# A routed expert loop that takes four lanes through each stage instead of two

## The chip, the cores and the metric

The kernel runs on one core of a Trainium2 chip. The metric is the time of one execution on the device in microseconds; the compared value is the median of several runs.

## The reference

One transformer layer on x of [2, 1024, 512]: attention with 32 query heads and 8 key heads, then a mixture of 64 routed experts with four chosen per token, and two shared experts. The feed-forward part is

```python
logits = flat @ router_w                                  # 2048 tokens, 64 experts
_, topk_idx = jax.lax.top_k(logits + router_bias, 4)
comb = ...                                                # renormalised softmax scores of the four
g = jax.nn.silu(jnp.einsum('nd,edf->nef', flat, wg))      # d = 512, f = 128
u = jnp.einsum('nd,edf->nef', flat, wu)
routed = jnp.einsum('ne,nef,efd->nd', comb, g * u, wd)
sg = jax.nn.silu(jnp.einsum('nd,sdh->nsh', flat, swg))    # two shared experts, h = 512 each
su = jnp.einsum('nd,sdh->nsh', flat, swu)
shared = jnp.einsum('nsh,shd->nd', sg * su, swd)
return routed + shared
```

## The kernel before

Each engine has its own program, written out by hand, and they meet in semaphores. Up to about 640 us the kernel does attention, the router and the shared experts for the first half of the tokens (`shared_ups`, `shared_down` for g = 0, 1). Then comes the routed loop, then the shared experts for the second half (g = 2, 3), while the routed results are fetched and mixed in.

**The lanes.** The choices (token, expert) are sorted by expert into tiles of 64 slots. There are 8 lanes of 24 tiles; a lane walks through its tiles and keeps its expert's weights while the expert stays the same. Two lanes form a pair (j = 0 to 3), side by side in the 128 partitions: each lane's weights are loaded as 64 columns of TensorE's array. Pair number n = 4 i + j runs from 0 to 95.

**The stages of pair n**, with the lines of the kernel before:
- GpSimd gathers its tokens (L919, `gather_tokens`, one indirect DMA), with slot numbers that ScalarE copied (L1097, `next_tokens`).
- TensorE turns them (`turn_slots`, L1443 and L1444, eight matmuls with full 128x128 weights); ScalarE copies the result (L1084, `turned_tokens`).
- TensorE multiplies by gate and up weights (`expert_up`, L1483, fp32, eight calls that are recorded as sixteen matmuls, with 64-column weights); ScalarE applies silu (L1089), VectorE the product (L1863, `expert_hidden`); ScalarE and VectorE split it into two fp16 parts (L1094 `e_high`, L1867 `e_low`).
- TensorE turns both parts (`turn_hidden`, L1492 and L1493, two matmuls with 128x128 weights); ScalarE copies (L1103, `hidden_turned`).
- The down weights are scaled and split: high part on ScalarE (L1109, `down_high`), low part on VectorE (L1873, `down_low`), in two buffers, `[:, j % 2]`. TensorE multiplies (`expert_down`, L1502, six matmuls with 64-column weights).
- VectorE takes the result out (L1880, L1882, `expert_y`) and GpSimd scatters it (L928, `scatter_y`, one indirect DMA, eight pairs behind the gather it follows).
- SyncE loads the weights of pair n + 4 into a buffer when up(n) and down_low(n) have read it (L645, L653).

**The order on the engines** is that of `expert_pairs` in each program. Before, a turning is one pair. TensorE: slots(n+1), hidden(n-2), up(n), down(n-2). ScalarE: turned(n+1), hidden_turned(n-2), next_tokens, down_high(n-1), silu(n), e_high(n). VectorE: expert_hidden(n), down_low(n-1), e_low(n), expert_y(n-2).

**Behind the loop** TensorE does `shared_up(g, hc)`, number k = 8 g + hc, 24 matmuls of 512 columns (L1360); from k = 17 on each waits for the hidden product k - 2 of VectorE (L1808). VectorE's order there is hidden(k), hidden_low(k-1), `mix(k - 16)` (L1911), where mix(t) waits for the routed results of token tile t, which SyncE fetches when all scatters have landed (L677).

## Time and profile before

| | us |
|---|---|
| Median of 3 runs | 1092.0 |
| Lowest, highest run | 1090.39, 1092.01 |
| The profiled execution's own time | 1091.62 |
| Its span, first to last instruction | 1089.8 |
| TensorE busy in the span | 1041.6 |
| VectorE, ScalarE, GpSimd busy | 848.8, 660.8, 532.5 |

The profile holds one execution. Times in it count from the span's start. A matmul's recorded length is that of its way through the array, so matmuls overlap in the records, and an engine that streams them looks busy throughout; starts, or the pieces of the chain, tell how fast the stream runs.

### The profile page before, as it was taken

Reading aid. Unit: us, or ns where it says so; the run is one execution under the profiler, and the core shown is the slowest. Engines: PE = TensorE matmul, PEld = TensorE weight load, DVE = VectorE, ACT = ScalarE, POOL = GpSimd, SP = SyncE. Lnnn points to the kernel's source line nnn. Section 1 sums busy time; section 2 is a strip of 40 time slices with the busy share of each in tenths; the row PEclk is TensorE's granted clock in tenths of the full one; section 3 lists DMA queues with packets and bytes.
Section 4 is the critical chain, followed back from the end, with each engine's and each line's share of the span. In section 5 each row is a group of like instructions: output and inputs, shape, how many; then the busy total and the mean of one; then the engine's idle time right before and its main releaser. Section 6 shows DMA issues by size and latency. Waiting matters only on the chain.

```text
span 1089.8 us, 29733 instructions
## 1 busy us (share of the span) xinstructions
PE 1041.6 (96%) x9832; PEld 504.8 (46%) x9833; DVE 848.8 (78%) x1331; ACT 660.8 (61%) x1334; POOL 532.5 (49%) x540
## 2 busy tenths in 40 slices
PE   5998899999999999899999999999999999989998
PEld 3534333333333333345544456666666666634443
DVE  6976999999999997398878927676777777768283
ACT  3323788888888889735620317777777777722020
POOL 6631143334333433435881946777777888610000
PEclk9998999999999999999999999999999999999999
DMA  9164111121112110044200077888887798558261
GB/s 260 26 170 107 43 49 46 46 73 58 44 45 73 58 44 25 6 150 155 78 1 1 2 270 247 270 265 280 304 288 238 231 317 293 177 194 268 67 226 39
DMA packets 72409, 150.66 MB, mean 138 GB/s; under 512 B 19460, under 2 KB 20868, under 8 KB 72356
## 3 DMA queue, kind: packets, MB, share of 16 engines
q1 hardware_dynamic: 52404, 109.51, 31.7%
q0 software_dynamic: 18304, 38.86, 10.9%
q10 hardware_dynamic: 1648, 1.58, 0.4%
q8 instruction: 35, 0.57, 0.2%
q14 instruction: 18, 0.15, 0.0%
HBM read 223.90 MB, written 38.80 MB: 241 GB/s over the span
## 4 chain that ended last, share of the span: by engine, by line
PE 71%; DVE 17%; issue 7%; ACT 3%; DMA 1%; POOL 1%; DVEq 0%; SPq 0%; ACTq 0%; POOLq 0%
PE PS L1483 17%; PE PS L1360 13%; PE PS L1465 8%; DVE maxes L1558 7%; PE PS L1502 6%; PE PS L1274 5%; PE PS L1223 4%; DVE max_low L1558 4%; PE PS L1155 4%; PE PS L1443 3%; PE PS L1252 3%; ACT att L1004 2%; PE PS L1327 2%; PE PS L1444 2%; DVE XT L1737 1%
## 5 line engine op out<-in xcount | busy, mean ns | idle before, releaser
L1004 ACT ACTIVATE att<-PS 128x512 f32<-128x512 f32 x576 | 312.6, 594 | 51.2 <-PE PS L1252 44.3
L1274 PE MATMUL PS<-att,v_head 128*32 128x256 f32 (+1 forms) x2560 | 178.2, 369 | 0.9 <-POOL att L793 0.9
L1558 DVE TENSOR_REDUCE maxes<-PS 128x2 f32<-128x1024 f32 (+2 forms) x192 | 172.6, 939 | 1.2 <-PE PS L1160 1.1
L1360 PE MATMUL PS<-XN,att 128*128 128x512 f16 x768 | 167.8, 380 | 0.3 <-ACT w_att L1066 0.3
L1558 DVE TENSOR_REDUCE max_low<-PS 128x2 f32<-128x1024 f32 x128 | 153.1, 1208 | 5.2 <-PE PS L1155 3.1
L919 POOL DMA_INDIRECT w_att<-xn_rows,idx x96 | 117.9, 1229 | 46.9 <-DVE w_att L1882 12.4
L793 POOL TENSOR_SCALAR_AFFINE_SELECT att<-att 128x512 f32<-128x512 f32 (+1 forms) x96 | 75.1, 790 | 127.8 <-ACT att L1004 127.0
L1252 PE MATMUL PS<-att 50*128 50x512 f16 (+1 forms) x640 | 111.7, 362 | 14.2 <-ACT att L1004 11.8
L1155 PE MATMUL PS<-att 48*128 48x512 f16 (+7 forms) x768 | 115.8, 325 | 9.0 <-DVE max_low L1558 3.9
L1360 PEld LDWEIGHTS PS<-XN,att 128*128 128x128 f16 x768 | 74.9, 98 | 91.2 <-issue 2.1
L1062 ACT ACTIVATE w_att<-PS 128x512 f32<-128x512 f32 x32 | 19.1, 598 | 158.3 <-PE PS L1360 158.3
L1863 DVE TENSOR_TENSOR w_att<-w_att,PS 128x128 f32<-128x128 f32 x96 | 27.6, 288 | 89.9 <-ACT w_att L1089 88.0
L1483 PE MATMUL PS<-XT,w_att 128*64 128x256 f32 x768 | 93.5, 385 | 0.2 <-issue 0.2
L1483 PE MATMUL PS<-ring,w_att 128*64 128x256 f32 x768 | 93.5, 385 | 0.1
L1155 PEld LDWEIGHTS PS<-att 48*128 48x128 f16 x768 | 35.7, 93 | 117.3 <-DVE maxes L1558 53.9
L1274 PEld LDWEIGHTS PS<-att,v_head 128*32 128x32 f32 x2560 | 55.9, 108 | 72.9 <-issue 48.4
L1465 PE MATMUL PS<-att,XT 128*128 128x512 f16 x384 | 83.7, 379 | 0.0
L1502 PE MATMUL PS<-XT,w_att 128*64 128x512 f16 x576 | 79.2, 382 | 1.9 <-DVE XT L1873 1.9
L1084 ACT ACTIVATE w_att<-PS 128x512 f32<-128x512 f32 x96 | 57.4, 597 | 39.0 <-PE PS L1444 33.7
L928 POOL DMA_INDIRECT choice_y<-w_att,idx_y x48 | 63.2, 1318 | 19.7 <-issue 8.3
L928 POOL DMA_INDIRECT choice_y<-att,idx_y x48 | 60.0, 1250 | 20.5 <-issue 8.6
L759 POOL TENSOR_TENSOR small<-small,recip 128x256 f32<-128x256 f32 x32 | 19.9, 621 | 93.5 <-DVE recip L1631 93.5
(205 smaller groups left out, 1827.5 us busy)
## 6 DMA issues: line engine op xcount, KB each, us to landing
ring<-in_L_ffn_wg_dram SPq DMA_DIRECT2D x96, 512.0 KB
XT<-in_L_ffn_wg_dram SPq DMA_DIRECT2D x96, 512.0 KB
ring<-in_L_ffn_wd_dram SPq DMA_DIRECT2D x96, 256.0 KB
XT<-in_L_ffn_wd_dram SPq DMA_DIRECT2D x96, 256.0 KB
ring<-choice_y SPq DMA_DIRECT2D x16, 1024.0 KB, 6.2
att<-q_stacks SPq DMA_DIRECT2D x60, 128.0 KB, 2.5
xn_rows<-ring SPq DMA_DIRECT2D x16, 256.0 KB, 3.1
out_dram<-X SPq DMA_DIRECT2D x16, 256.0 KB, 6.1
```

The costliest lines, as they stand in the source:

```text
L793: pool.affine_select(out=d, in_=d, compare_op=ALU.is_ge, fill=0.0, base=0, pattern=[[0, n], [1, P]], channel_multiplier=-1).then_inc(maske ...
L919: pool.indirect_dma_start(out=xg[:, j, :], out_offset=None, in_=xn2_rows[:, :], in_offset=bass.IndirectOffsetOnAxis(ap=idx[:, j:j + 1], ax ...
L928: pool.indirect_dma_start(out=choice_y[:, :], out_offset=bass.IndirectOffsetOnAxis(ap=idx_y[:, j:j + 1], axis=0), in_=result[j], in_offset ...
L1004: act.activation(probs[:, n0 % RING, u * BANK:(u + 1) * BANK], bank((2 * n0 + u) % EXP_BANKS), ACT.Exp, scale=HD ** -0.5 / QK_SCALE ** 2). ...
L1155: mm = pe.matmul(PS[:, to:to + n], q_max[b][rows, t * P:(t + 1) * P], k_max[b][rows, first:first + n], start=True, stop=lo is not None)
L1252: mm = pe.matmul(PS[:, at:at + 2 * qn], k_exp[b][rows, kt * P:(kt + 1) * P], q_exp[b][rows, 2 * q0:2 * (q0 + qn)] .rearrange("p (t h q) -> ...
L1274: mm = pe.matmul(PS[32 * r:32 * r + 32, at:at + qn], v_head[b][:, kt, :], probs[:, (NS * b + s) % RING, a:a + qn], start=s in (0, NS0), st ...
L1360: mm = pe.matmul(bank(2 * (n % 2) + k), shared_w[:, 2 * k + w, C * s + c, at:at + P], v[:, c, tokens], start=(c == 0 and w == 0 and v is x ...
L1465: mm = pe.matmul(bank(4 + t % 2), v[:, hc, (t % 4) * P:(t % 4 + 1) * P], swd_w[:, w, hc, :], start=(hc == 0 and w == 0 and v is hidden_hi) ...
L1483: mm = pe.matmul(PS[l * SUB:(l + 1) * SUB, at:at + 2 * F], xgt[:, j % 2, c * P + l * SUB:c * P + (l + 1) * SUB], lane_up[2 * j + l][:, :, ...
L1502: mm = pe.matmul(PS[l * SUB:(l + 1) * SUB, (4 + j % 2) * BANK:(5 + j % 2) * BANK], hg[:, j % 2, v * P + l * SUB:v * P + (l + 1) * SUB], w[ ...
L1558: last = dve.reduce_max(out, src, AXX)
```

## The change

The unit of `expert_pairs` becomes two pairs, a and a + 1, on TensorE, ScalarE and VectorE. TensorE turns the slots of a + 2 and a + 3, then both hidden parts of a - 2 and a - 1, then does both ups of a and a + 1 and both downs of a - 2 and a - 1. Slots 0 and 1 are turned ahead of the loop. The split down weights have four buffers, `[:, j]`, which lie in the first half of x_hi and x_lo (tile XN), whose tokens the shared experts have used by then; the waits for a free buffer go from e_down n - 1 to n - 3. `next_tokens` asks for pair n + 6, not n + 5. On ScalarE, down_high(a) ends a turning and down_high(a - 1) stands behind the two hidden_turned at its start. On VectorE both down_low of the turning before come first. After the last up and down of the loop, TensorE does the first shared block, `shared_up(EARLY, 0)`, ahead of the last turn_hidden of 94 and 95; `shared_ups` for g = 2 then begins with its second block. The programs of GpSimd and SyncE are untouched.

The diff, cut to its core:

```diff
...
         pair_down = [carve(arena, at, [P, 2, D])[0]
 -        down_hi, down_lo = carve_all(flat_xt, 2 * W, *[([P, 2, 2 * D], F16)] * 2)
+        down_hi, down_lo = x_hi[:, :, 0:2 * D], x_lo[:, :, 0:2 * D]
         xg, xgt, yb, sg, ht, hg = carve_all(w_att, 0, ([P, 4, 2 * D], F16), ([P, 2, D], FP32), ([P, 2, D], FP32),
                                             ([P, 2, P], FP32), ([P, 2, P], FP32), ([P, 2, 2 * P], F16))
         ht_hi, ht_lo = carve_all(w_att, 4 * D + 2 * D + 2 * D + 6 * P, ([P, 2, P], F16), ([P, 2, P], F16))
...
             def down_high(n, j, i):
                 act.wait_ge(pair_down_in[j], 32 * (i + 1))
 
-                wait(act, e_down, n - 1)
-                act.activation(down_hi[:, j % 2, :], pair_down[j][:, :, :].rearrange("p l d -> p (l d)"), ACT.Copy,
+                wait(act, e_down, n - 3)
+                act.activation(down_hi[:, j, :], pair_down[j][:, :, :].rearrange("p l d -> p (l d)"), ACT.Copy,
                                scale=W_SCALE).then_inc(down_hi_done, 1)
 
-            def expert_pairs(i, first, last):
-                for j in range(JP):
-                    n = JP * i + j
-                    if not (last and j == JP - 1):
-                        turned_tokens(n + 1, j + 1)
-                    if not (first and j < 2):
-                        hidden_turned(n - 2, (j - 2) % JP)
-                    if not last:
-                        next_tokens(i + 1 + (j + 1) // JP, (j + 1) % JP)
-                    if not (first and j < 1):
-                        down_high(n - 1, (j - 1) % JP, i if j else i - 1)
-                    silu(n, j)
-                    e_high(n, j)
+            def expert_pairs(i, first, turns, gathers):
+                for a in range(0, JP, 2):
+                    both = (a, a + 1)
+                    if not (first and a == 0):
+                        for j in both:
+                            hidden_turned(JP * i + j - 2, (j - 2) % JP)
+                        down_high(JP * i + a - 1, (a - 1) % JP, i if a else i - 1)
+                    for j in both:
+                        n = JP * i + j
+                        silu(n, j)
+                        if a < turns:
+                            turned_tokens(n + 2, j + 2)
+                        if a < gathers:
+                            next_tokens(i + 1 + (j + 2) // JP, (j + 2) % JP)
+                        e_high(n, j)
+                    down_high(JP * i + a, a, i)
 
             act.wait_ge(table_ready, 1)
             for j in range(JP):
                 next_tokens(0, j)
-            turned_tokens(0, 0)
-            next_tokens(1, 0)
-            expert_pairs(0, True, False)
-            with act.Fori(1, LANE_TILES - 1) as i:
-                expert_pairs(i, False, False)
-            expert_pairs(LANE_TILES - 1, False, True)
-            hidden_turned(PAIRS - 2, JP - 2)
-            hidden_turned(PAIRS - 1, JP - 1)
+            for j in range(2):
+                turned_tokens(j, j)
+                next_tokens(1, j)
+            expert_pairs(0, True, JP, JP)
+            expert_pairs(1, False, JP, JP)
+            with act.Fori(2, LANE_TILES - 2) as i:
+                expert_pairs(i, False, JP, JP)
+            expert_pairs(LANE_TILES - 2, False, JP, JP - 2)
+            expert_pairs(LANE_TILES - 1, False, JP - 2, 0)
+            for j in (JP - 2, JP - 1):
+                hidden_turned(PAIRS - JP + j, j)
             down_high(PAIRS - 1, JP - 1, LANE_TILES - 1)
 
             act.wait_ge(e_down, PAIRS)
...
                     if t == 4 * EARLY - 1:
                         pe.wait_ge(table_ready, 1)
                         pe.wait_ge(ident_h_set, 1)
-                        turn_slots(0, 0, 0)
+                        for n in range(2):
+                            turn_slots(n, n, 0)
                     if t == 4 * EARLY:
                         pe.wait_ge(yb_ready, PAIRS)
                     if t >= 2:
...
                     for l in range(2):
                         mm = pe.matmul(PS[l * SUB:(l + 1) * SUB, (4 + j % 2) * BANK:(5 + j % 2) * BANK],
                                        hg[:, j % 2, v * P + l * SUB:v * P + (l + 1) * SUB],
-                                       w[:, j % 2, l * D:(l + 1) * D], start=(v == 0 and w is down_hi), stop=v == 1)
+                                       w[:, j, l * D:(l + 1) * D], start=(v == 0 and w is down_hi), stop=v == 1)
                 mm.then_inc(e_down, 1)
 
             def expert_pairs(i, first, last):
-                for j in range(JP):
-                    n = JP * i + j
-                    if not (last and j == JP - 1):
-                        turn_slots(n + 1, j + 1, i)
-                    if not (first and j < 2):
-                        turn_hidden(n - 2, (j - 2) % JP)
-                    expert_up(n, j, i)
-                    if not (first and j < 2):
-                        expert_down(n - 2, (j - 2) % JP)
+                for a in range(0, JP, 2):
+                    both = (a, a + 1)
+                    if not (last and a == JP - 2):
+                        for j in both:
+                            turn_slots(JP * i + j + 2, j + 2, i)
+                    if not (first and a == 0):
+                        for j in both:
+                            turn_hidden(JP * i + j - 2, (j - 2) % JP)
+                    for j in both:
+                        expert_up(JP * i + j, j, i)
+                    if not (first and a == 0):
+                        for j in both:
+                            expert_down(JP * i + j - 2, (j - 2) % JP)
 
 
             expert_pairs(0, True, False)
             with pe.Fori(1, LANE_TILES - 1) as i:
                 expert_pairs(i, False, False)
             expert_pairs(LANE_TILES - 1, False, True)
-            turn_hidden(PAIRS - 2, JP - 2)
-            turn_hidden(PAIRS - 1, JP - 1)
-            expert_down(PAIRS - 2, JP - 2)
-            expert_down(PAIRS - 1, JP - 1)
+            pe.wait_ge(xgt_ready, PAIRS)
+            pe.wait_ge(x_lo_ready, 4 * (EARLY + 1))
+            shared_up(EARLY, 0)
+            for j in (JP - 2, JP - 1):
+                turn_hidden(PAIRS - JP + j, j)
+            for j in (JP - 2, JP - 1):
+                expert_down(PAIRS - JP + j, j)
 
             for g in range(EARLY, 4):
-                shared_ups(g, g % EARLY)
+                shared_ups(g, 1)
                 shared_down(g)
 
         @block.vector
...
 
             def down_low(n, j):
                 dve.wait_ge(down_hi_done, n + 1)
-                wait(dve, e_down, n - 1)
-                dve.scalar_tensor_tensor(out=down_lo[:, j % 2, :], in0=pair_down[j][:, :, :].rearrange("p l d -> p (l d)"),
-                                         scalar=W_SCALE, in1=down_hi[:, j % 2, :], op0=ALU.mult, op1=ALU.subtract)\
+                wait(dve, e_down, n - 3)
+                dve.scalar_tensor_tensor(out=down_lo[:, j, :], in0=pair_down[j][:, :, :].rearrange("p l d -> p (l d)"),
+                                         scalar=W_SCALE, in1=down_hi[:, j, :], op0=ALU.mult, op1=ALU.subtract)\
                    .then_inc(down_lo_done, 1)
 
             def expert_y(n, j, i):
...
                 dve.wait_ge(e_down, n + 1)
                 dve.tensor_scalar(result[j], bank(4 + j % 2), 1 / (H_SCALE * W_SCALE), None, ALU.mult).then_inc(yb_ready, 1)
 
-            def expert_pairs(i, first, last):
-                for j in range(JP):
-                    n = JP * i + j
-                    expert_hidden(n, j)
-                    if not (first and j < 1):
-                        down_low(n - 1, (j - 1) % JP)
-                    e_low(n, j)
-                    if not (first and j < 2):
-                        expert_y(n - 2, (j - 2) % JP, i if j >= 2 else i - 1)
-
-            expert_pairs(0, True, False)
-            expert_pairs(1, False, False)
-            with dve.Fori(2, LANE_TILES - 1) as i:
-                expert_pairs(i, False, False)
-            expert_pairs(LANE_TILES - 1, False, True)
-            down_low(PAIRS - 1, JP - 1)
-            expert_y(PAIRS - 2, JP - 2, LANE_TILES - 1)
-            expert_y(PAIRS - 1, JP - 1, LANE_TILES - 1)
+            def expert_pairs(i, first):
+                for a in range(0, JP, 2):
+                    later = not (first and a == 0)
+                    n, before = JP * i + a, i if a else i - 1
+                    if later:
+                        down_low(n - 2, (a - 2) % JP)
+                        down_low(n - 1, (a - 1) % JP)
+                    expert_hidden(n, a)
+                    e_low(n, a)
+                    expert_hidden(n + 1, a + 1)
+                    if later:
+                        expert_y(n - 2, (a - 2) % JP, before)
+                    e_low(n + 1, a + 1)
+                    if later:
+                        expert_y(n - 1, (a - 1) % JP, before)
+
+            expert_pairs(0, True)
+            expert_pairs(1, False)
+            with dve.Fori(2, LANE_TILES) as i:
+                expert_pairs(i, False)
+            for j in (JP - 2, JP - 1):
+                down_low(PAIRS - JP + j, j)
+            for j in (JP - 2, JP - 1):
+                expert_y(PAIRS - JP + j, j, LANE_TILES - 1)
 
             def mix(t):
```

TensorE in the steady loop, before: behind the last matmul of turn_slots (L1443, L1444) come turn_hidden (L1492, L1493), up (L1483), down (L1502), and the next slots.

```order
L1444 MATMUL PS<-ident_h,w_att 128x128
L1492 MATMUL PS<-ident_h,w_att 128x128
L1493 MATMUL PS<-ident_h,w_att 128x128
L1478 REGISTER_ALU
L1483 MATMUL PS<-XT,w_att 64x256 x8
L1502 MATMUL PS<-XT,w_att 64x512 x6
L1438 ISA
L1443 MATMUL PS<-ident_h,w_att 128x128
```

The same place after, where turn_slots is L1449 and L1450, turn_hidden L1499 and L1500, up L1490, down L1509:

```order
L1450 MATMUL PS<-ident_h,w_att 128x128
L1499 MATMUL PS<-ident_h,w_att 128x128
L1500 MATMUL PS<-ident_h,w_att 128x128
L1499 MATMUL PS<-ident_h,w_att 128x128
L1500 MATMUL PS<-ident_h,w_att 128x128
L1490 MATMUL PS<-XT,w_att 64x256 x16
L1509 MATMUL PS<-XN,w_att 64x512 x12
L1531 REGISTER_ALU
L1531 COMPARE_AND_BRANCH
L1449 MATMUL PS<-ident_h,w_att 128x128
```

Two ups stand in a row, and two downs; between one change of the weights' width and the next there is twice the work.

ScalarE in the steady loop, before: turned_tokens (L1084), hidden_turned (L1103), next_tokens (L1097), down_high (L1109), silu (L1089), e_high (L1094), one pair.

```order
L1084 ACTIVATE w_att<-PS 128x512
L1103 ACTIVATE w_att<-PS 128x256
L1097 ISA
L1097 ACTIVATE idx<-small 128x1
L1109 ACTIVATE XT<-XT 128x1024
L1089 ACTIVATE w_att<-PS 128x128
L1094 ACTIVATE w_att<-w_att 128x128
```

The same lines after, one turning of two pairs:

```order
L1103 ACTIVATE w_att<-PS 128x256 x2
L1109 ACTIVATE XN<-ring 128x1024
L1089 ACTIVATE w_att<-PS 128x128
L1081 REGISTER_ALU
L1084 ACTIVATE w_att<-PS 128x512
L1097 ISA
L1097 ACTIVATE idx<-small 128x1
L1094 ACTIVATE w_att<-w_att 128x128
L1089 ACTIVATE w_att<-PS 128x128
```

Turned_tokens has moved behind silu and ahead of e_high, and both hidden_turned and one down_high stand at the start of the turning.

TensorE at the loop's end, before: the last up (L1483), the downs, both turn_hidden, and then the shared blocks (L1360).

```order
L1483 MATMUL PS<-XT,w_att 64x256 x8
L1502 MATMUL PS<-XT,w_att 64x512 x6
L1492 MATMUL PS<-ident_h,w_att 128x128
L1493 MATMUL PS<-ident_h,w_att 128x128
L1492 MATMUL PS<-ident_h,w_att 128x128
L1493 MATMUL PS<-ident_h,w_att 128x128
L1502 MATMUL PS<-XT,w_att 64x512 x12
L1360 MATMUL PS<-XN,att 128x512 x216
```

The same place after, where the shared blocks are L1366:

```order
L1490 MATMUL PS<-XT,w_att 64x256 x16
L1509 MATMUL PS<-XN,w_att 64x512 x12
L1366 MATMUL PS<-XN,att 128x512 x24
L1499 MATMUL PS<-ident_h,w_att 128x128
L1500 MATMUL PS<-ident_h,w_att 128x128
L1499 MATMUL PS<-ident_h,w_att 128x128
L1500 MATMUL PS<-ident_h,w_att 128x128
L1509 MATMUL PS<-XN,w_att 64x512 x12
L1366 MATMUL PS<-XN,att 128x512 x192
```

One shared block of 24 matmuls now stands between the last downs and the last turn_hidden.

## Rows read from the trace of the kernel before

**Rows 1.** The page, busy us of an engine, share of the span, instructions.
```profile
PE 1041.6 (96%) x9832; PEld 504.8 (46%) x9833; DVE 848.8 (78%) x1331; ACT 660.8 (61%) x1334; POOL 532.5 (49%) x540
```

**Rows 2.** Table by stretch, the routed loop: length, busy (x instructions), clock, DMA.
```profile
core 0: us, PE busy (x) PEld busy (x) DVE busy (x) ACT busy (x) POOL busy (x), PEclk, DMA share, GB/s
655.00:950.00 295.00, 294.69 (x2943) 183.13 (x2940) 209.88 (x459) 229.53 (x551) 228.04 (x181) 1.00 0.79 267
```

**Rows 3.** Chain of work that ended last, in the loop: start, us, what.
```profile
943.17 0.18 PE PS L1443
943.35 0.06 PE PS L1444
...
943.86 1.88 PE PS L1483 x16
945.73 0.65 PE PS L1502 x6
...
947.06 1.88 PE PS L1483 x16
...
947.86 1.08 PE PS L1483 x10
```

**Rows 4.** Timeline of ScalarE, in the loop and at its end: start, us, line.
```profile
759.35 0.28 ACT L1089 ACTIVATE w_att<-PS 128x128 f32<-128x128 f32 x1
759.98 0.31 ACT L1094 ACTIVATE w_att<-w_att 128x128 f16<-128x128 f32 x1 [0.35 <-DVE w_att L1863]
760.55 0.60 ACT L1084 ACTIVATE w_att<-PS 128x512 f32<-128x512 f32 x1 [0.27 <-PE PS L1444]
761.05 0.38 ACT L1103 ACTIVATE w_att<-PS 128x256 f16<-128x256 f32 x1
761.41 1.06 ACT L1109 ACTIVATE XT<-XT 128x1024 f16<-128x1024 f32 x1
...
954.93 0.28 ACT L1089 ACTIVATE w_att<-PS 128x128 f32<-128x128 f32 x1 [0.56 <-PE PS L1483]
```

**Rows 5.** Timeline of VectorE, in the loop.
```profile
758.06 0.68 DVE L1882 TENSOR_SCALAR att<-PS 128x512 f32<-128x512 f32 x1
759.66 0.29 DVE L1863 TENSOR_TENSOR w_att<-w_att,PS 128x128 f32<-128x128 f32 x1 [0.92 <-ACT w_att L1089]
759.86 1.22 DVE L1873 SCALAR_TENSOR_TENSOR XT<-ring,XT 128x1024 f16<-128x1024 f32 x1
761.00 0.28 DVE L1867 SCALAR_TENSOR_TENSOR w_att<-w_att 128x128 f16<-128x128 f32 x1
...
761.26 0.68 DVE L1882 TENSOR_SCALAR w_att<-PS 128x512 f32<-128x512 f32 x1
```

**Rows 6.** Timeline of GpSimd, in the loop.
```profile
757.73 1.04 POOL L928 DMA_INDIRECT choice_y<-att,idx_y  x1 [0.31 <-issue]
759.16 1.03 POOL L919 DMA_INDIRECT w_att<-xn_rows,idx  x1 [0.39 <-DVE att L1882]
760.49 1.48 POOL L928 DMA_INDIRECT choice_y<-att,idx_y  x1 [0.31 <-issue]
```

**Rows 7.** Waits by engine, 670 to 940 us: total, times, longest.
```profile
ACT XT L1109 <- DMA ring<-in_L_ffn_wd_dram: 0.2, 1, 0.2
```

**Rows 8.** Timeline of TensorE at the loop's end.
```profile
954.72 0.82 PE L1502 MATMUL PS<-XT,w_att 128*64 128x512 f16 x6
...
956.92 0.23 PE L1492 MATMUL PS<-ident_h,w_att 128*128 128x128 f16 x1 [1.17 <-DVE w_att L1867]
...
959.89 1.49 PE L1502 MATMUL PS<-XT,w_att 128*64 128x512 f16 x6 [1.91 <-DVE XT L1873]
961.31 14.01 PE L1360 MATMUL PS<-XN,att 128*128 128x512 f16 x61
```

**Rows 9.** Timeline of VectorE behind the loop.
```profile
961.42 0.69 DVE L1882 TENSOR_SCALAR att<-PS 128x512 f32<-128x512 f32 x1 [0.87 <-PE PS L1502]
...
970.54 3.12 DVE L1911 SCALAR_TENSOR_TENSOR X<-ring,small,X 128x512 f32<-128x512 f32 x4 [1.66 <-DMA ring<-choice_y]
973.58 0.68 DVE L1808 SCALAR_TENSOR_TENSOR w_att<-PS,w_att 128x512 f32<-128x512 f32 x1
```

1 line of the change is left out of this document (removed).

## The prediction

> **What bounds the kernel now.** I read the page first: TensorE is busy for 1041.6 us of the 1089.8 us span [rows 1]. A share over the whole span says little of one stage, so the second view is the table by stretch. In the routed loop, 655 to 950 us, TensorE shows 294.7 us busy of 295 at a granted clock of 1.00, while VectorE has 210, ScalarE 230 and GpSimd 228 [rows 2]. The third view is the chain of work that ended last. There the loop is nothing but TensorE, pair after pair, 3.20 us apart (943.86 to 947.06) [rows 3].
>
> "Busy" is not "working", and the chain shows how much is not. In the chain a piece ends where the matmul ends, so a piece of one matmul is its share of the stream. Ten up matmuls in mid-stream take 1.08 us, thus 0.216 us for two (the two lanes run side by side). Sixteen should take 1.73 us, but where they follow the square 128x128 matmuls of turn_slots and turn_hidden they take 1.88: 0.15 us extra. The six of expert_down, which follow up with three waits of their own, take 0.65 = 3 x 0.216: nothing extra. The first square matmul after them takes 0.18 us where the nine others take 0.06: 0.12 us extra [rows 3]. So each pair pays 0.27 us for two changes: square to half-width (64-column) weights, and back. It does not pay for waits: turn_hidden has two waits of its own and goes on at 0.06. The loop's minimum is 3.21 - 0.27 = 2.94 us a pair.
>
> **What the change does to TensorE in the loop.** It removes no matmul. Two pairs share one turning: slots, slots, hidden, hidden, up, up, down, down. Each turning has one change to half width and one back, so 48 turnings have 48 double changes where 96 pairs had 96. That takes away 48 x 0.27 = 13.0 us, if TensorE never waits; the turning is then 2 x 3.207 - 0.27 = 6.14 us.
>
> **Does it wait?** I lay the other engines against a turning, with t = 0 at the start of up(a). TensorE: up(a) to 1.78, up(a+1) to 3.50, both downs to 4.80, both slots from 4.90 to 5.82, turn_hidden(a) at 5.82, turn_hidden(a+1) at 5.93, next turning at 6.14. Durations are those of [rows 4, 5]; ScalarE and VectorE start an instruction some 0.1 us before the recorded end of the one before; a releaser costs 0.03 (silu ends at 759.63, expert_hidden starts at 759.66); and silu starts 0.2 us after the matmul that follows its up (954.72 on TensorE in rows 8, 954.93 on ScalarE).
> - The chain that now matters: silu(a+1) at 3.70, turned_tokens(a+3) 3.89, the index copy 4.40, e_high(a+1) 4.51 to 4.82, e_low(a+1) 4.94 to 5.22. TensorE wants it at 5.93. It has 0.7 us of room. expert_y(a-2) stands ahead of e_low(a+1), but waits only for the first down (ends 4.15) and starts at 4.35.
> - ScalarE behind it: down_high(a) 4.73 to 5.79, two hidden_turned from 6.13 to 6.79, down_high(a+1) to 7.76; silu(a+2) is released at 8.11. Room 0.35 us.
> - VectorE: down_low(a+1) is released at 7.79 and runs to 9.01, so expert_hidden(a+2), queued behind it, starts 0.5 us late (8.92 instead of 8.42). e_high(a+2) follows at 9.24, and ScalarE would have waited until 9.83 for silu(a+3) anyway: nothing is passed on. down_low(a+1) itself is wanted at 10.28.
> - Slots(a+5) wait for turned_tokens(a+3), ready at 4.49, wanted at 5.37.
>
> So all waits keep some room and the stage stays TensorE's. The wait for down's buffers is gone with four of them, but it was not what bound anything: no row shows it.
>
> **GpSimd and the transfers.** GpSimd is the engine I trust least. A gather or scatter takes 1.03 to 1.04 us and 0.31 between two; a scatter over whose end expert_y runs takes 1.48 [rows 6]. It ends when expert_y ends: 761.97 against 761.94 (rows 5 and 6). Yet the scatter at 757.73 holds an expert_y wholly inside (758.06 to 758.74) and takes 1.04. So expert_y holds up only an end. Per turning: 4 x 1.34 = 5.36 us, plus at most two ends held, 0.45 each as in the row, 6.26. The two expert_y now end within 0.85 us of each other (5.03 and 5.87), so two ends, which are 1.34 apart, can hardly both be held: 5.8 us of 6.14. Next_tokens now asks for n+6 instead of n+5, so a gather late by 1 us still lands before it is turned. I take nothing for it.
>
> Weights: down_low(a) frees its buffer some 3.5 us later than now, so down weights have less lead. The one wait for them in the loop is 0.2 us [rows 7]. I take 0, and up to +3 us as the upper bound (the two busiest bursts losing 1.5 us each).
>
> **The start.** One more pair of slots stands ahead of up(0), which only moves work. But the first turning has no downs to cover the chain of ScalarE: slots(5) must wait for turned_tokens(3), which by the same calendar is ready 0.2 + 0.19 + 0.60 us after up(1), with 0.1 + 0.47 of slots(4) ahead of it: 0.5 us. The next up waits 0.2 us for turn_hidden(1). +0.7.
>
> **The end.** Before: TensorE waits 1.2 us for e_low(95) (recorded idle 1.17) and 1.9 us for down_low(95) (1.91) [rows 8]. After these the granted clock falls to half: the last six downs take 1.49 us where those at 954.72 take 0.82, +0.67, and the first 61 shared matmuls 14.01 where 61 x 0.216 + 0.16 = 13.3, +0.7. Together 4.5 us. After: shared_up(16), 24 matmuls of 0.216 = 5.2 us, fills the first wait. But ScalarE's down_high(95) stands behind both hidden_turned, and these now come after the shared block. From the last turn_hidden to the last expert_down it was 2.97 us (956.92 to 959.89); with one hidden_turned more it is 3.2, of which TensorE works 1.0. So 2.3 us of waiting are still there, 0.4 ahead of down(94) and 1.9 ahead of down(95), and with 0.3 for the shorter last turning it is 2.6.
>
> Then a new wait. Shared_up(19) needs hidden(17), which VectorE computes after mix(0), and mix(0) needs the last scatter. From the last expert_y's start (961.42) it is 9.1 us to mix(0) (970.54) and 12.2 to hidden(17) (973.58, ends 974.26) [rows 9]. After the change, with D the start of down(95), expert_y(95) starts at D + 0.84, and hidden(17) ends at D + 13.7 to 14.1 (0.4 if the scatter of 94 is in the way). TensorE meanwhile is one block further than before: it stands before shared_up(19) at D + 0.75 + 2 x 5.18 = 11.1. It waits 3.0 us there. VectorE catches up later: about 4.5 us of work per block against 5.2. Last, some 3 us of idle time halved the clock before at a cost of 1.4 us; I take that once more: +1.4.
>
> **Sum**, against the profiled execution's 1091.6 us (span 1089.8 and 1.8 around it): -13.0 in the loop, +0.7 at its start, -4.5 + 2.6 at its end, +3.0 at shared_up(19), +1.4 for the clock: -9.8, thus 1081.8 us. The runs' median, 1092.0, lies 0.4 above the profiled one.
>
> **Rivals.**
> 1. **The 0.27 belongs to the stages, not to the changes.** If each first matmul behind a stage's waits costs it, then up to up and slots to slots pay too and the loop gains nothing; -4.5 + 0.7 + 2.6 + 3.0 + 1.4 = +3.2 would leave 1095. Up to down and slots to hidden, with waits and no cost [rows 3], speak strongly against it.
> 2. **No wait at shared_up(19)**, or the clock holds: 1077 to 1080.4. The room is 3 us wide, so this needs transfers faster than the row's.
> 3. **Weights arrive late**: +1 to +3, 1083 to 1085. For it: shorter lead for down. Against: one wait of 0.2 us in 96 pairs [rows 7].
> 4. **GpSimd becomes the bound (slower).** If expert_y locks GpSimd out for all of its 0.68 us wherever it falls, a turning needs 5.36 + 2 x 0.68 = 6.72 us, 0.31 more than two pairs take now. It decides from 6.41 us on. 47 x 0.58 us above the forecast: 1109. For it: the held ends. Against: the row at 757.73. The Trainium skill (SBUF — State Buffer, "Who interferes with whom") says that one of VectorE and GpSimd takes the shared port pair for a whole instruction and the other fully blocks, which would be this rival; it also says that an instruction with at most one SBUF input outside the 2-port modes does not contend, and expert_y reads PSUM, which the held ends contradict.
> 5. **The change doesn't do what it says**: the rows of the order above show the new turning on each engine, so I give it nothing.
>
> **How the numbers follow.** Forecast 0.67, rival 2 0.12, rival 3 0.10, rival 1 0.05, rival 4 0.06. A run of this kernel can tell 0.2% (2.2 us) from no change. Forecast and rivals 2 and 3 are all faster: 0.89, of which I take 0.02 off for a partial rival 1. Slower: rivals 1 and 4 less a little, 0.09. Same: 0.04. The range reaches from rival 2's lower end, 1077, to 1087, which leaves out rivals 1 and 4 and takes in a loop that gains 8 instead of 13.
>
> **What would show it.** In the profile after: a first up piece of 1.88 us followed by a second of 1.73 in the chain; turnings 6.14 us apart; no idle time of TensorE in the loop; the page's PE busy time down by about 13 us; an idle time of 1.9 us before the last expert_down released by down_low; one of about 3 us before the fourth shared block, released by VectorE. It is wrong if the second up or the second slots show the extra 0.1 to 0.15, if turn_hidden(a+1) waits for e_low, or if gathers and scatters fill 6.4 us of a turning.

## The result, and the profile of the changed kernel

The changed kernel takes 1155.99 us (median of 6 runs, 1149.34 to 1157.18) where the kernel before takes 1092.78 (6 runs on the same chip): a ratio of 1.0565, 95% interval 1.0545 to 1.0585. It is 63 us slower. The forecast was 1081.8 us with 0.87 for "faster". The profiled execution took 1155.8 us, its span is 1154.1.

The page: busy us of each engine, and the chain that ended last by engine and by line.

```profile
PE 1051.9 (91%) x9833; PEld 517.6 (45%) x9833; DVE 857.9 (74%) x1331; ACT 648.6 (56%) x1333; POOL 535.6 (46%) x540
...
PE 49%; DVE 19%; DMA 12%; issue 11%; ACT 4%; POOL 4%; POOLq 0%; DVEq 0%; SPq 0%; ACTq 0%
```

TensorE's share falls from 96% [rows 1] to 91%, and transfers now hold 12% of the chain; before, it was 1%. The table by stretch says where (columns as in [rows 2]; the loop's last up ends 64 us later, at 1018.5 instead of 954.9, so the stretch is longer):

```profile
655.00:1000.00 345.00, 293.32 (x2816) 188.18 (x2814) 209.35 (x438) 209.11 (x532) 220.89 (x175) 0.94 0.69 227
655.00:700.00 45.00, 39.84 (x415) 26.01 (x412) 29.61 (x64) 31.26 (x81) 28.36 (x23) 1.00 0.72 231
850.00:900.00 50.00, 44.88 (x464) 29.29 (x463) 34.41 (x72) 34.10 (x87) 36.77 (x29) 1.00 0.63 214
```

Before, no engine but TensorE mattered in the loop: busy 294.7 of 295 us at a clock of 1.00 [rows 2]. Now it idles 52 of 345 us, and its mean clock is 0.94. The waits of TensorE and GpSimd from 655 to 1010 us (engine, tile, line, what ended them; total, times, longest) name the cause:

```profile
POOL w_att L919 <- ACT idx L1097: 57.3, 17, 7.1
...
PE PS L1449 <- DMA w_att<-xn_rows,idx: 51.3, 23, 3.6
...
POOL choice_y L928 <- DVE att L1896: 22.4, 18, 1.8
```

L1449 is turn_slots, and it waits 23 times for gathered rows, 51.3 us in all. No row of the kernel before shows one such wait. Nearly all of it comes once per turn of the loop: 18 of the 19 waits of over 1.2 us stand ahead of the slots of every fourth pair, the second slots of a turning. TensorE around two of these waits:

```profile
755.68 0.25 PE L1449 MATMUL PS<-ident_h,w_att 128*128 128x128 f16 x1 [2.75 <-DMA w_att<-xn_rows,idx]
...
756.47 5.36 PE L1490 MATMUL PS<-ring,w_att 128*64 128x256 f32 x32
...
764.29 3.67 PE L1490 MATMUL PS<-XT,w_att 128*64 128x256 f32 x32
...
772.86 0.24 PE L1449 MATMUL PS<-ident_h,w_att 128*128 128x128 f16 x1 [3.03 <-DMA w_att<-xn_rows,idx]
...
773.65 5.36 PE L1490 MATMUL PS<-ring,w_att 128*64 128x256 f32 x32
```

A wait of 2.75 or 3.03 us costs more than itself: the 32 up matmuls behind it take 5.36 us instead of 3.67, since the granted clock has fallen to its lower level for part of them. From 756.47 to 773.65 it is 17.2 us for four pairs, where 12.83 were usual before and 12.28 forecast: 3.03 for the wait, 1.69 for the slow up, the remaining 0.2 in the first slots behind the wait.

Why the rows come late is seen on GpSimd (start, us, line; idle time before and what ended it), with VectorE's two down_low (L1887) beneath:

```profile
761.48 1.02 POOL L919 DMA_INDIRECT w_att<-xn_rows,idx  x1 [3.48 <-ACT idx L1097]
764.08 2.04 POOL L928 DMA_INDIRECT choice_y<-att,idx_y  x1 [1.57 <-DVE att L1896]
766.42 1.72 POOL L919 DMA_INDIRECT w_att<-xn_rows,idx  x1 [0.31 <-issue]
768.44 1.01 POOL L928 DMA_INDIRECT choice_y<-att,idx_y  x1 [0.31 <-issue]
```

```profile
764.00 1.23 DVE L1887 SCALAR_TENSOR_TENSOR XN<-ring,XN 128x1024 f16<-128x1024 f32 x1
766.01 1.23 DVE L1887 SCALAR_TENSOR_TENSOR XN<-ring,XN 128x1024 f16<-128x1024 f32 x1 [0.79 <-ACT XN L1109]
```

The gather that TensorE waits for at 772.86 is the one of 766.42. It stands in GpSimd's queue behind the scatter of 764.08, which waited 1.57 us for expert_y. The program lets it go with expert_y of its own pair, number 26, which ends at 763.21; the scatter starts 0.87 us later, much as a gather that waits for its indices starts 0.84 us after their copy. The scatter takes 2.04 us instead of 1.03, and the gather 1.72. Both end 0.9 us after a down_low does (765.23 and 767.24), of which more below. The chain of waits through this place:

```profile
763.47 0.61 DVE att L1896
764.08 0.48 POOL choice_y L928
...
766.42 6.32 DMA w_att<-xn_rows,idx
...
772.86 0.24 PE PS L1449
```

(The profile puts the scatter down to expert_y(27), the last to end before it; by the program it isn't waited for.) So from the gather's start to the landing it is 6.32 us, 4.6 of them after GpSimd is done with it. From 767.5 to 769.5 us the 16 DMA engines served nothing but SyncE's queue with the weights (queues in that stretch: packets, MB, share; the software queue of GpSimd has no line):

```profile
q1 hardware_dynamic: 155, 0.57, 99.5%
```

I call the time from a gather's start on GpSimd to the start of its slots on TensorE its lead. In the kernel before it is 10.3 us (median of the starts in the records; least 8.9). In the changed one it is 9.4, 7.0, 7.3 and 6.2 us for the four pairs of a turn of the loop (medians from pair 8 to 91; least 4.0). TensorE's own wait is part of that: without it, the fourth pair has 3.4 us.

The landing itself didn't change. Each gather completes with 16 signals, and both traces hold their times. From a gather's start to the last of them (gathers of the loop with at least 15 of the 16 on record) it is 2.7 to 7.2 us, median 4.8, in the kernel before (79 gathers) and 2.7 to 7.2, median 4.5, in the changed one (85). 10.3 us covered all of that, and 3.4 covers little of it. The room that hid the landing is gone.

Behind the loop the profile is close to the forecast:

```profile
PE PS L1366 <- DVE w_att L1822: 2.4, 1, 2.4
PE PS L1509 <- DVE XN L1887: 1.6, 1, 1.6
PE PS L1509 <- issue: 0.4, 1, 0.4
```

### The profile page after: what moved, and what is told of

Its sections match the earlier page's. It is cut to its first block, busy times and chain, and to the rows that moved or that the text cites. A ratio compares the mean times of both kernels' runs of the same rounds, so it can differ in the third digit from the quotient of the medians.

```text
span 1154.1 us, 29668 instructions
## 1 busy us (share of the span) xinstructions
PE 1051.9 (91%) x9833; PEld 517.6 (45%) x9833; DVE 857.9 (74%) x1331; ACT 648.6 (56%) x1333; POOL 535.6 (46%) x540
## 4 chain that ended last, share of the span: by engine, by line
PE 49%; DVE 19%; DMA 12%; issue 11%; ACT 4%; POOL 4%; POOLq 0%; DVEq 0%; SPq 0%; ACTq 0%
DMA w_att<-xn_rows,idx 11%; PE PS L1490 10%; PE PS L1366 10%; DVE maxes L1572 6%; PE PS L1472 6%; PE PS L1280 5%; PE PS L1229 4%; DVE max_low L1572 4%; PE PS L1161 4%; PE PS L1258 3%; ACT att L1004 2%; PE PS L1333 2%; DVE att L1896 2%; PE PS L1449 1%; POOL w_att L905 1%
## 5 line engine op out<-in xcount | busy, mean ns | idle before, releaser
L1366 PE MATMUL PS<-XN,att 128*128 128x512 f16 x768 | 167.4, 379 | 2.7 <-DVE w_att L1822 2.4
L919 POOL DMA_INDIRECT w_att<-xn_rows,idx x96 | 113.8, 1185 | 90.4 <-ACT idx L1097 61.3
L1887 DVE SCALAR_TENSOR_TENSOR XN<-XT,XN 128x1024 f16<-128x1024 f32 x48 | 58.8, 1224 | 77.9 <-ACT XN L1109 77.9
L1366 PEld LDWEIGHTS PS<-XN,att 128*128 128x128 f16 x768 | 74.6, 98 | 93.1 <-DVE w_att L1822 2.9
L1062 ACT ACTIVATE w_att<-PS 128x512 f32<-128x512 f32 x32 | 19.1, 598 | 152.5 <-PE PS L1366 150.3
L1490 PE MATMUL PS<-ring,w_att 128*64 128x256 f32 x768 | 104.7, 434 | 0.0
L1449 PE MATMUL PS<-ident_h,w_att 128*128 128x128 f16 x384 | 53.9, 227 | 52.5 <-DMA w_att<-xn_rows,idx 52.2
L928 POOL DMA_INDIRECT choice_y<-att,idx_y x48 | 70.3, 1464 | 38.6 <-DVE att L1896 22.4
L1490 PE MATMUL PS<-XT,w_att 128*64 128x256 f32 x768 | 88.2, 382 | 0.0
L1103 ACT ACTIVATE w_att<-PS 128x256 f16<-128x256 f32 x96 | 31.6, 381 | 82.8 <-PE PS L1500 82.8
L1490 PEld LDWEIGHTS PS<-ring,w_att 128*64 128x64 f32 x768 | 60.6, 157 | 36.3 <-issue 15.3
L1887 DVE SCALAR_TENSOR_TENSOR XN<-ring,XN 128x1024 f16<-128x1024 f32 x48 | 58.8, 1225 | 22.9 <-ACT XN L1109 22.9
```

The costliest lines, as they stand in the source:

```text
L919: pool.indirect_dma_start(out=xg[:, j, :], out_offset=None, in_=xn2_rows[:, :], in_offset=bass.IndirectOffsetOnAxis(ap=idx[:, j:j + 1], ax ...
L928: pool.indirect_dma_start(out=choice_y[:, :], out_offset=bass.IndirectOffsetOnAxis(ap=idx_y[:, j:j + 1], axis=0), in_=result[j], in_offset ...
L1366: mm = pe.matmul(bank(2 * (n % 2) + k), shared_w[:, 2 * k + w, C * s + c, at:at + P], v[:, c, tokens], start=(c == 0 and w == 0 and v is x ...
L1490: mm = pe.matmul(PS[l * SUB:(l + 1) * SUB, at:at + 2 * F], xgt[:, j % 2, c * P + l * SUB:c * P + (l + 1) * SUB], lane_up[2 * j + l][:, :, ...
L1887: dve.scalar_tensor_tensor(out=down_lo[:, j, :], in0=pair_down[j][:, :, :].rearrange("p l d -> p (l d)"), scalar=W_SCALE, in1=down_hi[:, j ...
```

## The experiments

**The chips.** The runs below were made on six other chips, and on all of them the kernel before takes 1176 to 1189 us, not 1092. In its trace from such a chip (c_before) the code outside the loop takes the same time within 1 us; the loop is 84 us longer, with a cause of its own (experiment 4). There, SyncE, ScalarE and TensorE stop for moments that no semaphore explains; below I call these the stops. So every number is compared with the kernel before on its own chip, and where I speak of a cause, with TensorE's waits in the trace rather than with the total alone.

| kernel | edit | us | kernel before there | ratio, 95% |
|---|---|---|---|---|
| c_before | none | 1176.5 | 1177.2 | one run |
| c_after | the change | 1164.6 | 1177.2 | 0.988 to 0.994 |
| x1_gathers_first | change, GpSimd's order | 1150.0 | 1177.7 | 0.975 to 0.978 |
| x3_early | change, early indices | 1182.3 | 1177.7 | 1.002 to 1.005 |
| x2_early_and_first | both of these | 1151.4 | 1177.7 | 0.976 to 0.979 |
| x2_again | the same | 1151.0 | 1175.9 | 0.975 to 0.983 |
| x5_short_down_low | change, short down_low | 1146.7 | 1175.9 | 0.972 to 0.982 |
| x4_before_short_lead | before, later gathers | 1133.6 | 1177.7 | 0.961 to 0.965 |
| u_before | before, loop written out | 1153.8 | 1188.1 | 0.970 to 0.974 |
| u_after | change, loop written out | 1170.4 | 1188.1 | 0.984 to 0.988 |
| u_early_and_first | x2, loop written out | 1149.0 | 1188.1 | 0.965 to 0.969 |
| nw_before, nw_after | no weights' transfers | 1153.9, 1150.3 | 1187.9 | 0.972, 0.969 |
| ng_before, ng_after | no gathers | 1092.0, 1081.9 | 1187.9 | 0.920, 0.911 |
| hg_before, hg_after | rows of half the bytes | 1187.7, 1164.4 | 1188.7 | 0.999, 0.979 |

Even the sign of the change isn't the same everywhere. On the one of these chips where both kernels ran as they are, the changed one is 0.9% faster (c_after); on another, with the loop written out in both, it is 1.4% slower (u_after 1170.4, u_before 1153.8). What follows explains the 63 us of the first chip, where none of the experiments ran.

**1. Is it the gathers at all?** Both kernels without the gathers of the loop (those for the first four pairs stay).

```diff
                 wait_alone(pool, idx_set, n + 1, pool_passed)
+                if not (isinstance(i, int) and i == 0):
+                    return
                 pool.indirect_dma_start(out=xg[:, j, :], ...
...
-                pe.wait_ge(xg_in[k % JP], 16 * (i + k // JP + 1))
+                pe.wait_ge(xg_in[k % JP], 16)
```

> The changed kernel with its weights' transfers, but without the gathers behind the first four (the same rows are computed on again; the output is not the reference's). Theory (lead): TensorE waits for no rows; whatever is left over nw_after is the weights' own: stops, late down weights. On a chip with stops 1100 to 1140, against 1163 to 1170 for the changed kernel there. Rival (turning): 1155 or more, since another wait stands in the place.

> The kernel before without the same gathers. No row of its trace shows TensorE waiting for one, so it keeps its time (1174 to 1188 on a chip with stops) unless the stops come from gathers and weights together, then 1090 to 1130.

Measured: 1081.9 and 1092.0 us. Without gathers the kernel before takes what it took on the first chip, and the changed one 10.1 us less; the forecast's sum was 9.8 less and 1081.8. It came out lower than I expected of ng_after (1100 to 1140), since the stops go with the gathers too. The chain of ng_after in the loop is the one that the prediction drew:

```profile
858.43 1.29 PE PS L1511 x12
859.72 0.18 PE PS L1451
...
860.96 3.60 PE PS L1492 x32
864.57 1.29 PE PS L1511 x12
...
867.10 3.60 PE PS L1492 x32
```

From up to up it is 867.10 - 860.96 = 6.14 us. 32 up matmuls take 3.60 us, that is 1.88 + 1.73 - 0.01, twelve downs 1.29 = 2 x 0.65, and the first square matmul still 0.18. And TensorE waits nowhere in the loop but once, 0.4 us, at its start; these are all its waits from 655 us to the end:

```profile
PE PS L1368 <- DVE w_att L1824: 2.3, 1, 2.3
PE PS L1511 <- DVE XN L1889: 1.6, 1, 1.6
PE PS L1511 <- issue: 0.4, 1, 0.4
PE PS L1451 <- ACT w_att L1086: 0.4, 1, 0.4
```

So the rival that ScalarE's and VectorE's chains in the merged turning are too long falls, and so does the one that the width changes cost nothing. From up(2) to up(94) TensorE needs 282.06 us, against 295.01 in ng_before: 12.95 less for 46 turnings.

**2. What makes the gather late?** Three suspects stand in the rows: its place in GpSimd's queue, down_low's hold, and the weights' transfers. Each is taken away alone. First the order:

```diff
             with pool.Fori(2, LANE_TILES) as i:
-                for j in range(JP):
-                    gather_tokens(i, j)
-                    scatter_y(i - 2, j)
+                for a in range(0, JP, 2):
+                    for j in (a, a + 1):
+                        gather_tokens(i, j)
+                    for j in (a, a + 1):
+                        scatter_y(i - 2, j)
```

> The changed kernel, with one edit: GpSimd issues both gathers of a turning and then both scatters, where it issued gather, scatter, gather, scatter. Theory (lead): the loop is long because the gather for every fourth pair starts only 6.0 us before TensorE wants its rows (10.3 us in the kernel before), since it stands behind a scatter that waits for expert_y. Out of that place it starts some 1.5 to 2.5 us sooner and the wait of 2.75 to 3.03 us once per four pairs gets shorter or goes: 1095 to 1135 us, with gathers then bound by the index copies of ScalarE. Rival (turning): ScalarE's and VectorE's chains of the merged turning are too long in themselves and the gather is only what ends last; then another wait stands in its place and the time stays above 1145. Rival (transfers): the rows come late because the weights' transfers hold the DMA engines, however early they are asked for; then under 15 us are gained.

Then the index copies (x3_early), and both (x2_early_and_first):

```diff
+                    if a < gathers:
+                        for j in both:
+                            act.wait_ge(xg_turned, JP * i + j + 3)
+                            next_tokens(i + 1 + (j + 2) // JP, (j + 2) % JP)
                     ...
-                        if a < gathers:
-                            next_tokens(i + 1 + (j + 2) // JP, (j + 2) % JP)
```

> The changed kernel, with one edit: ScalarE copies the indices of both gathers of a turning right behind hidden_turned, before down_high, instead of one behind each turned_tokens (some 2 to 4 us sooner). Order on GpSimd as in the changed kernel. Theory (lead): the gather that TensorE waits for still stands behind the scatter that waits for expert_y, so it starts no sooner: 1140 to 1157 us. If the index copy alone were what is late, under 1110.

> The changed kernel, with both edits: indices copied early, and both gathers ahead of both scatters on GpSimd. Theory (lead): every gather then starts 8 us or more before its slots, TensorE no longer waits in the loop, the turning is the forecast 6.14 us and the kernel takes 1078 to 1088 us. Rival (turning): above 1120, with waits for turned_tokens, e_low or down_low in the gather's place. Rival (width change costs nothing): the waits go but the turning is 6.4 us, 1092 to 1096.

> The same kernel as x2_early_and_first (indices copied early, both gathers ahead of both scatters), once more, because on the chip of the first four runs the kernel before itself took 1177.7 us instead of 1092, and SyncE, ScalarE and TensorE stalled together in the loop with no semaphore missing. On a chip where the kernel before takes 1092 us the theory (lead) expects 1078 to 1088, the rival (turning) above 1120, the rival (down weights late, since their buffers are freed later) 1090 to 1110 with waits of down_high for pair_down_in.

Then down_low with 256 of its 1024 columns, the rest left out:

> The changed kernel, with down_low cut from 1024 to 256 columns (the rest of the low part is left out, so down's correction is incomplete; the output is not the reference's). In the traces of both kernels a gather or scatter that GpSimd starts while down_low runs on VectorE ends 0.89 us after down_low's end (76 and 88 cases, 0.86 to 0.91), else it takes 1.03. In the changed kernel a scatter takes 2.04 and the gather behind it 1.72 us in this way. Theory (hold): with a down_low of some 0.35 us both take 1.03 to 1.3, the gather for every fourth pair starts about 1.5 us sooner relative to its slots, and 20 to 45 us of the 63 come back: 1110 to 1136. If the holds cost nothing on the path: 1150 to 1157.

And both kernels without the weights' transfers of the loop (SyncE's loop is left out, and TensorE and ScalarE wait for the first load only):

> The kernel before without the weights' transfers of the routed loop behind its first four pairs (192 lanes keep the weights of the first eight; the output is not the reference's); gathers, scatters and all arithmetic stay. Theory (transfers): the steps of 0.73 us in which SyncE, ScalarE and TensorE stop come with the weights' traffic, so there are none, and the loop is TensorE's at 3.21 us a pair: 1088 to 1094 us. Rival (gathers and scatters make the stops, or the chip is slower): 1150 to 1190.

> The changed kernel without the same transfers. If the prediction's sum was right and only the gathers' landing behind the weights' bursts was left out of it, a gather now lands within 2 us, the turning is 6.14 us, and the kernel takes 1078 to 1085 us, 0.988 to 0.993 of nw_before. If the width change cost nothing, 1.000 to 1.005 of it. If the order of gathers and scatters alone (without a burst) makes TensorE wait: above 1100, with the wait at every fourth slots.

The changed kernel on such a chip, for comparison:

> The changed kernel itself on the same chip as the kernel before: which ratio has the change on such a chip (1.0565 on the first)? Theory (lead): it waits for every fourth gather here too, so it lies at x3_early's ratio, 1.00 to 1.01, since the stalls that lengthen the kernel before fall into its waits. Rival (the stalls add to both): 1.05 to 1.06, about 1240 us.

What each does to TensorE's wait for rows, from 655 to 1010 us. In this order: c_after, x1_gathers_first, x3_early, x5_short_down_low, nw_after.

```profile
PE PS L1449 <- DMA w_att<-xn_rows,idx: 30.4, 16, 3.4
```

```profile
PE PS L1451 <- DMA w_att<-xn_rows,idx: 4.4, 5, 1.8
```

```profile
PE PS L1452 <- DMA w_att<-xn_rows,idx: 29.7, 17, 3.2
```

```profile
PE PS L1449 <- DMA w_att<-xn_rows,idx: 13.0, 12, 2.4
```

```profile
PE PS L1447 <- DMA w_att<-xn_rows,idx: 4.2, 5, 1.7
```

x2_early_and_first has none. x1, x2 and x3 ran on one chip, c_after, x5 and nw_after on one each, so only large differences count. The wait of 30.4 us goes to 4.4 when gathers no longer stand behind a scatter, is untouched (29.7) when only the indices come earlier, goes to 13.0 with a short down_low, and to 4.2 without the weights. Leads and landings, measured as above but with TensorE's wait taken off the lead, say why:

| kernel | shortest of the four median leads | landing (gathers on record) | waits for rows |
|---|---|---|---|
| c_after | 3.8 | 2.8 to 6.1 (23) | 30.4 |
| x1_gathers_first | 6.0 | 3.5 to 6.1 (3) | 4.4 |
| x2_early_and_first | 7.8 | 2.8 to 6.4 (23) | none |
| x3_early | 3.0 | 2.8 to 5.8 (30) | 29.7 |
| x5_short_down_low | 4.6 | 3.4 to 5.4 (12) | 13.0 |
| nw_after | 3.8 | 2.7 to 3.5 (29) | 4.2 |

The order and the short down_low lengthen the lead; without the weights the lead stays and the landing gets shorter (not within 2 us, as I had expected, but within 3.5). Half the bytes of each row do some of it too: hg_after of experiment 4 has 11.7 us of waits for rows. So none of the three is "the" cause: the shortest lead had shrunk to less than a landing takes, and each takes a part. The order is the one that can be mended for nothing. The indices were never what was late: x3_early leaves the waits for rows as they were. It is even 1.3% slower than the change, by their ratios to the kernel before (1.0035 and 0.991), with 20.9 us of waits for down_low, and it missed the range expected (1140 to 1157).

The totals don't follow the waits. x1 gained 14.5 us on c_after (ratios 0.977 and 0.991), x2 with no wait for rows at all no more than x1, and nw_after, expected at 1078 to 1085, took 1150. None of x1, x2, x5 and nw_after reached the range that the theory of the lead (or of the hold) had given it, and c_after, expected at 1.00 to 1.01 of the kernel before, came out at 0.991. The ranges of the rivals by which another wait stands in the place, above 1145 and above 1120, fit x1 and x2. In the traces it does: TensorE waits for down_low in x2_early_and_first, and for turned_tokens in nw_after.

```profile
PE PS L1514 <- DVE XN L1892: 34.2, 22, 1.9
```

```profile
PE PS L1447 <- ACT w_att L1082: 37.7, 35, 1.5
```

In ng_after, the same turning without gathers, neither is there, so the merged turning doesn't bring these waits by itself. In both traces they stand beside waits of ScalarE that no semaphore explains, 96 and 87 us (experiment 4).

**3. Does a shorter lead hurt the kernel before?** Its gathers are asked for one pair and most of a turning later:

```diff
-                    if not last:
-                        next_tokens(i + 1 + (j + 1) // JP, (j + 1) % JP)
                     if not (first and j < 1):
                         down_high(n - 1, (j - 1) % JP, i if j else i - 1)
                     silu(n, j)
+                    if not last:
+                        next_tokens(i + 1, j)
                     e_high(n, j)
...
-            next_tokens(1, 0)
```

> The kernel before, with one edit: next_tokens asks for the pair n+4 behind silu(n), instead of n+5 ahead of down_high, so each gather starts some 5 to 6 us before its slots instead of 10.3. Nothing else changes. Theory (lead): TensorE waits for rows in the stretches where weights come in a burst, 15 to 60 us in all: 1107 to 1150. Rival (turning): a gather lands 1 to 4 us after its start, as its packets in the kernel before look, so nothing changes: 1090 to 1094.

In the trace the leads are 5.7 to 6.5 us and the landings 3.4 to 6.8 (16 gathers on record), and waits for rows appear where c_before has none:

```profile
PE PS L1442 <- DMA w_att<-xn_rows,idx: 12.3, 15, 1.9
```

So it isn't the merged turning that makes a gather late: with this lead it is late in the kernel before too. The rival's landing of 1 to 4 us was read off the packets too hastily; the completions say 2.7 to 7.2. The total went the other way, 1133.6 against 1177.7 us; that it lies in the range expected is chance, since the range was reckoned from 1092.

**4. What makes the loop longer on these chips?** The kernel before, traced there:

> The kernel before itself, once more, for its trace: on the two chips of the first six runs it took 1176 to 1178 us, where its runs shown ahead of the prediction took 1092. Theory (chip): the loop alone is longer, and SyncE, ScalarE and TensorE stall together there with no semaphore missing, 80 us in all. Rival: TensorE waits for gathers or weights there (slower transfers), which the packets' durations would show.

ScalarE in its loop (start, us, line, idle time before):

```profile
741.88 1.05 ACT L1109 ACTIVATE XT<-XT 128x1024 f16<-128x1024 f32 x1
745.96 0.28 ACT L1089 ACTIVATE w_att<-PS 128x128 f32<-128x128 f32 x1 [3.02 <-remote]
```

This silu waits for an up that TensorE had streamed 3 us before; no semaphore accounts for it. SyncE comes forward in steps of about 0.7 us from 742.2 to 744.4 (742.22, 742.95, 743.69, 744.40), a few instructions at each, and TensorE's 16 up matmuls of 744.03 take 2.95 us instead of 1.95. VectorE and GpSimd show no such steps there. On the first chip neither trace has a wait of ScalarE that no semaphore explains. I tried the loop instruction (the routed loop written out on every engine):

> The kernel before with its routed loop written out on all five engines (no loop instruction there; the same instructions in the same order). On the chips of the last runs the kernel before takes 1176 us, and in its loop SyncE, ScalarE and TensorE stop for steps of 0.73 us at the same places of each turn of the loop, with no semaphore missing. Theory (loop): these stops come with the loop instruction, so the written out loop has none and takes 1088 to 1096 us here. Rival (load): they come with the traffic of the transfers, and it stays at 1170 to 1180.

> The changed kernel with its routed loop written out in the same way. Theory (lead), if the stops go: 1145 to 1160 us, as on the first chip, with waits for every fourth gather and for little else. If the waits for gathers on the first chip were caused by the loop instruction too: 1078 to 1088.

> The changed kernel with indices copied early and both gathers of a turning ahead of both scatters, and its routed loop written out. Theory (lead): each gather starts 8 us or more before its slots, TensorE doesn't wait for rows, the turning is 6.14 us and the kernel takes 1076 to 1086 us. Rival (turning): above 1120, with another wait in the gather's place. Rival (down weights late): 1090 to 1110, with down_high waiting for its transfer.

The stops stay: ScalarE's waits of this kind add up to 113 us in c_before, 98 in u_before and 88 in nw_before. But each of the two edits takes 34 us off, of the 96 by which the kernel before is longer on those chips, and why isn't shown; u_before (1153.8) fits neither range set for it, 1088 to 1096 without stops and 1170 to 1180 with them, and nw_before (1153.9) fits that of the rival. So neither is what the stops need. Gathers are: ng_before has no such wait of ScalarE, and takes 1092.0 us. u_after (1170.4 us) and u_early_and_first (1149.0) missed their ranges, 1145 to 1160 and 1076 to 1086, which took the stops to be gone. Last, whether it goes by their bytes; each gathered row cut to 1024 bytes:

> The kernel before with each gathered row cut to its first half, 1024 bytes instead of 2048 (as many rows; the low halves of the tokens are not fetched and the rows are others, so the output is not the reference's). Without gathers the kernel took 1092.0 us on a chip where it takes 1187.9 with them. If that cost goes by the bytes gathered: about half of it comes back, 1130 to 1145 us. If it goes by the gathers and their rows: 1165 to 1190.

> The changed kernel with the same cut. Without gathers it took 1081.9 us, with whole ones 1163 to 1170 on such chips. By the bytes: 1115 to 1130, and TensorE's waits for rows (30.4 us in c_after) go to under 10. By the rows: 1150 to 1170 with waits as in c_after.

1187.7 us, as with whole rows: the extra time goes by the gathers or their rows, not by bytes. What in a gather stops three other engines on some chips and not on another stays open. One regularity may help whoever goes on: ScalarE's waits that no semaphore explains (655 to 1010 us) mostly grow with the lead of the gathers. The largest row of them in c_before, where the leads are 11.6 to 13.5 us, and in x4, where they are 5.7 to 6.5:

```profile
ACT w_att L1089 <- remote: 106.8, 38, 4.8
```

```profile
ACT w_att L1089 <- remote: 33.2, 18, 3.5
```

All rows of this kind together are 113 us in c_before, 96 in x2 (7.8 to 9.7), 75 in c_after (5.3 to 8.6), 66 in x1 (6.2 to 6.9), 50 in x4 and 47 in x5 (4.9 to 6.9); x3 with 110 (4.4 to 9.7) and nw_after with 87 (5.3 to 8.5) fit less well. That could be why x4 is the fastest here of the kernels that leave nothing out. It is a correlation; no run shows a cause.

**Versions that beat both kernels.** On these chips x1, x2 and u_early_and_first beat both, and so does x4, the kernel before with later gathers: at 0.963 it is the fastest of all that leave nothing out, though nothing speaks for it on the first chip, where there are no stops. x1 is c_after's code with one loop in another order, 0.977 of the kernel before against 0.991. On a chip like the first one it wasn't tried. What speaks for it there is its trace (4.4 us of waits for rows instead of 30.4) and ng_after (10 us are there to be had); that it would come near ng_after's 1081.9 on such a chip is argued, not shown. With landings of up to 7.2 us there, its shortest lead of 6.0 would still leave some waits, where the 7.8 of x2_early_and_first would cover all.

## Why the prediction was wrong

**The step that failed** is in "GpSimd and the transfers": "Next_tokens now asks for n+6 instead of n+5, so a gather late by 1 us still lands before it is turned. I take nothing for it." Three things were wrong in it.

- It counted the request, not the lead. Slots(n+6) also stand a turning earlier. From my own calendar it could have been read: expert_y(n-2) ends at 5.03 us of the turning, the scatter behind it at 6.1, so gather(n+7) starts at 6.4, and its slots stand at 11.04 + 0.47 = 11.5. That leaves 5.1 us, where there had been 10.3. Measured it is 3.4, with TensorE's wait taken off (6.2 with it): the calendar lacks the 0.87 us from the end of expert_y to the start of the scatter that waits for it, and 1.0 us by which down_low holds the scatter; the two together would leave 3.2.
- It named nothing queued behind the new place of expert_y. Before, the scatter behind gather(n+5) was that of pair n-3, whose result was there (idle 0.31 to 0.39 us before each in [rows 6]). Now GpSimd waits for it, 22.4 us for the results kept in att alone, and a gather is queued behind.
- It took the landing for granted. No row that I showed has it, because TensorE never waited for a gather; but the trace of the kernel before holds the completions, 2.7 to 7.2 us after the start, and the prediction should have read them. Measured in the chain of the changed kernel, it is 6.3 us from the start, 4.6 from GpSimd's end.

The price, from up(2) to up(94): 51.3 us of waits for rows, 16.6 us in 11 of the 46 up blocks, which run partly at the lower clock (1.69 of them at 756.47), and some 6 in other places of the same turnings. Together 74 us, as from 1081.8 to 1155.8. On the first chip this sum is argued from its trace; the link from the gathers to the time is shown by ng_after and ng_before on another.

**A reading that was wrong.** In [rows 5, 6] I took the scatter of 1.48 us to be held by expert_y, as both ended together (761.97 and 761.94). It was down_low: that of 759.86 ends at 761.08, and the scatter 0.89 us later. In the trace before, 89 of 192 gathers and scatters start while a down_low runs, and end 0.86 to 0.91 us after its end; in the changed one it is 76, and all others take 0.98 to 1.19. Where the gather or scatter starts first (by 0.10 us or more in these two traces), neither takes longer than alone, and x5, with a down_low of 0.42 us, has gathers of 1.03 and scatters of 1.02 (medians). So the sum over a turning (5.8 of 6.14 us) was harmless and the place was not: the change puts two down_low right behind the two expert_y, exactly when a scatter and the critical gather start, 1.0 and 0.7 us. The Trainium skill (SBUF — State Buffer, "Who interferes with whom") says that an instruction with at most one SBUF input outside the 2-port modes doesn't contend with GpSimd, and that one with two SBUF inputs does contend with a GpSimd instruction that reads SBUF. Read so, it fits this trace (expert_y reads PSUM and holds nothing; down_low reads two tiles of SBUF and lengthens the scatter by 1.0 us); I wrote that the held ends contradict it, and that was my misreading of the row.

**Term by term**, by ng_after against ng_before and the rows of the changed kernel:

- Loop, -13.0: -12.95 over 46 of the 48 turnings, at 6.14 us each. Right. What the four buffers of down are worth by themselves no run shows.
- No wait in the loop from ScalarE's and VectorE's chains: right in ng_after, with rooms of 0.35 to 0.7 us.
- Start, +0.7: some 1.3. Up(2) starts 2.3 us later than in ng_before, with 1.0 us of work moved ahead of it. Of this 0.8 is a wait for the second gather inside the shared block (646.05 in ng_after, which keeps the first four), again a gather, and 0.4 the wait for turned_tokens that I put at 0.5.
- End, -4.5 + 2.6: waits of 0.4 and 1.6 us (forecast 0.4 and 1.9).
- Shared_up(19), +3.0: 2.4 us (2.3 in ng_after). Hidden(17) ends 13.6 us after down(95) starts; forecast 13.7 to 14.1.
- Clock behind that wait, +1.4: nothing, so this term was wrong. The 84 matmuls of the chain of the changed kernel behind it take 84 x 0.216 + 0.16 us, at full speed:

```profile
1041.09 0.69 DVE w_att L1822
...
1041.83 18.30 PE PS L1366 x84
```

- Weights late: not seen in the changed kernel. But their traffic holds the gathers.

The loop and the start are read against ng_before, on another chip; the end, shared_up(19) and the clock are rows of the changed kernel on the first.

Rival 4 had the right engine and the wrong mechanism: GpSimd has time to spare (wait for indices, 57.3 us), and it is the order of what it does, not the amount, that costs. None of the five rivals had the gathers' landing; the slower side got 0.09, all of it for other reasons.
